# Linear attention in a fused decoder: row-by-row waits at its end, later unpackings, the context's low parts all on VectorE, and another order at its start

## The reference

```
qkv = silu(h @ qkv_w.T)                      # 32 heads of 128, q, k, v
scores = (q @ k.T) * decay                   # within and across blocks of 32 tokens
attn = scores @ v                            # 32 heads
xf = attn * rsqrt(mean(attn*attn) + 1e-5)    # over all 4096 columns of a token
x = x + (sigmoid(h @ gate_w.T) * norm_w * xf) @ out_w.T
...
x = x + cross_attention(layernorm(x), ctx, ctx, Wq, Wk, Wv, Wo)
x = x + layernorm(x) @ unpack_3bit(weight_q3, weight_norm).T + bias
```

## Time and profile before

| | us |
|---|---|
| median of 3 runs | 2436.48 |
| lowest and highest | 2434.27, 2437.48 |
| the profiled execution | 2437.57 |
| its span | 2435.0 |
| PE busy | 2323.7 (95%) |
| DVE busy | 1467.1 (60%) |
| ACT busy | 1020.6 (42%) |
| POOL busy | 914.8 (38%) |

### The profile page before, as it was taken

The page is one execution under the profiler, slowest core; times in us unless marked ns, Lnnn a source line. Parts: engine busy times, 40 slices in busy tenths (PEclk is TensorE's granted clock), DMA queues, the critical chain, the costliest instruction groups (busy, mean ns, idle before and its releaser), DMA issues.

```text
span 2435.0 us, 39959 instructions
## 1 busy us (share of the span) xinstructions
PE 2323.7 (95%) x12939; PEld 1972.7 (81%) x12939; DVE 1467.1 (60%) x3222; ACT 1020.6 (42%) x2447; POOL 914.8 (38%) x674
## 2 busy tenths in 40 slices
PE   6999899999999999998979999999999999987898
PEld 5788788888888888887768888888888888876556
DVE  7444644444444444446676666666666666658777
ACT  2111344444444444443244444444444444433784
POOL 3444523222222322221444444444444444413462
PEclk8999999999999999999989999999999999998999
DMA  3210212111111211110111111111111111120000
GB/s 118 78 43 26 96 53 83 55 52 65 55 52 52 81 56 52 65 56 27 55 52 46 45 45 45 45 45 45 45 45 45 46 46 45 45 95 18 1 1 35
DMA packets 39377, 125.26 MB, mean 51 GB/s; under 512 B 4888, under 2 KB 7320, under 8 KB 39328
## 3 DMA queue, kind: packets, MB, share of 16 engines
q1 hardware_dynamic: 39328, 124.64, 14.9%
HBM read 120.43 MB, written 4.19 MB: 51 GB/s over the span
## 4 chain that ended last, share of the span: by engine, by line
PE 81%; DVE 7%; POOL 5%; issue 4%; ACT 3%; DMA 0%; ACTq 0%; POOLq 0%; DVEq 0%; SPq 0%
PE pj L762 14%; PE pj L763 14%; PE pj L764 14%; PE ou L762 6%; PE ou L764 6%; PE ou L763 6%; PE tp L762 3%; PE tp L764 2%; PE tp L763 2%; PE sc L1101 2%; PE pv L952 2%; PE sc L936 2%; PE pv L1113 2%; POOL w_lo L550 1%; POOL sums_lo L644 1%
## 5 line engine op out<-in xcount | busy, mean ns | idle before, releaser
L550 POOL TENSOR_TENSOR w_lo<-raw,w_hi 128x1024 fp32r<-128x1024 f32 x100 | 240.6, 2407 | 802.2 <-ACT w_hi L1462 762.8
L762 PE MATMUL ou<-w_hi,act_hi 128*128 128x512 f32 x684 | 278.2, 407 | 11.8 <-DVE act_lo L2381 4.4
L1879 DVE TENSOR_TENSOR x<-x,ou 128x512 f32<-128x512 f32 x192 | 130.7, 683 | 247.6 <-PE ou L764 247.3
L763 PE MATMUL ou<-w_lo,act_hi 128*128 128x512 f32 x684 | 269.3, 394 | 0.0
L764 PE MATMUL ou<-w_hi,act_lo 128*128 128x512 f32 x684 | 269.2, 394 | 0.0
L762 PE MATMUL pj<-xt_hi,w_hi 128*128 128x512 f32 x622 | 254.2, 409 | 10.3 <-DVE values L2361 3.7
L763 PE MATMUL pj<-xt_lo,w_hi 128*128 128x512 f32 x622 | 244.7, 393 | 0.0
L764 PE MATMUL pj<-xt_hi,w_lo 128*128 128x512 f32 x622 | 244.4, 393 | 0.0
L1538 ACT ACTIVATE queries_keys<-pj 128x512 f32<-128x512 f32 x128 | 76.5, 598 | 244.8 <-PE pj L764 244.8
L762 PEld LDWEIGHTS ou<-w_hi,act_hi 128*128 128x128 f32 x684 | 130.0, 190 | 51.5 <-issue 18.5
L629 POOL TENSOR_TENSOR w_lo<-raw,w_hi 128x768 fp32r<-128x768 f32 x48 | 88.7, 1848 | 184.8 <-ACT w_hi L1599 184.6
(11 more groups left out here) (363 smaller groups left out, 6333.3 us busy)
## 6 DMA issues: line engine op xcount, KB each, us to landing
raw<-in_l1a_w SPq DMA_DIRECT2D x80, 512.0 KB, 3.4
raw<-in_l0x_w SPq DMA_DIRECT2D x64, 512.0 KB, 4.3
side<-in_side SPq DMA_DIRECT2D x32, 512.0 KB, 4.0
raw<-in_ffn_w SPq DMA_DIRECT2D x15, 512.0 KB, 3.4
raw<-in_l0f_w SPq DMA_DIRECT2D x6, 512.0 KB, 3.8
raw<-in_l1x_w SPq DMA_DIRECT2D x6, 512.0 KB, 3.4
raw<-in_taylor_w SPq DMA_DIRECT2D x5, 512.0 KB, 8.3
decay<-in_decay SPq DMA_DIRECT2D x16, 129.0 KB, 2.1
```

The lines of the kernel that those rows point to most:

```text
L550: pool.tensor_tensor(WL[:, s, :], RAW[:, s, :], f32(WH[:, s, :]), ALU.subtract).then_inc(w_ready[s], 1)
L762: pe.matmul(out, wh, xh, start=first, stop=False)
L763: pe.matmul(out, wh, xl, start=False, stop=False)
L1879: dve.tensor_tensor(dst, dst, ou[bank][:], ALU.add).then_inc(x_done, 1)
```

## The change

It has two places. **At the end**, PE's last odd half gets an order of its own: R4 stands behind V(0), R5 behind V(2), R6 behind V(3), R7 behind O(3), where all four stood behind V(3) and O(3) before. The tail's V(n) waits for its own value row instead of for R7, and `sums(0)` for R6. ACT and DVE follow with their parts; ACT rounds the context's pieces among and behind the value rows. DVE makes all four low parts of the context, behind R7's product, and POOL none. Of the unpackings, 0 and 1 stay in the odd half; 2 and 3, 4 and 5, 6 and 7 go behind the tail's `gated` of its batch rows 0, 1 and 2. SP starts the context's loads after the 63rd gate sigmoid instead of the 64th. DVE waits for the last gate weighting before it overwrites the third probabilities.

**At the start**, POOL makes the low sums of slot 3 first and begins `first_weights(1)` only when DVE has made two of the four low parts of the tokens (la_tlo); the clearing of the sums of squares goes behind slot 2's split. DVE normalises batch rows 6 and 7 one step earlier. ACT does `sums_hi(3, 0)` between the roundings of batch rows 6 and 7.

On SP and POOL:

```diff
-            sp.wait_ge(la_gs, 4 * HG)
+            sp.wait_ge(la_gs, 4 * HG - 1)
...
             pool.wait_ge(ou_full, OU["l0f"] + B)
+            sums_lo(3, 0)
+            pool.wait_ge(la_tlo, 2)
             first_weights(1)
-            pool.wait_ge(ln_x, 4 * B)
+            sums_lo(4, 0)
+            split(2, SLOT["l1a"][2])
             pool.memset(SQ[:], 0.0).then_inc(y_zero, 1)
-            sums_lo(3, 0)
-            split(2, SLOT["l1a"][2])
-            sums_lo(4, 0)
...
-            for c in range(2):
-                ctx_lo_again(c)
```

On PE, in `l1a_odd` and in the tail:

```diff
+                if not new:
+                    V(0)
+                    R(4)
+                    O(0)
+                    V(1)
+                    scores_l1a(i, 1, (la_fm, values + 1))
+                    O(1)
+                    V(2)
+                    R(5)
+                    O(2)
+                    V(3)
+                    R(6)
+                    O(3)
+                    R(7)
+                    return
...
-                    weighted(HG - 1, 1, n, event(HG - 1, "R7"))
+                    weighted(HG - 1, 1, n, event(HG - 1, f"R{4 + n}"))
...
             tail("V", 0)
+            pe.wait_ge(la_fm, event(HG - 1, "R6") + 1)
             sums(0)
```

On ACT, in `l1a_odd` and at the start:

```diff
                     V(0)
+                    row_value(i, 4)
                     V(1)
                     V(2)
-                    row_value(i, 4)
+                    row_value(i, 5)
+                    whole_ctx(0)
                     V(3)
-                    row_value(i, 5)
-                    act.wait_ge(c2_in, 16 * KC)
-                    for c in range(KC):
-                        act.activation(CH[:, c, :], CR[:, c, :], ACT.Copy).then_inc(c2_hi, 1)
-                        if c in (1, 3):
-                            row_value(i, 6 + c // 2)
+                    row_value(i, 6)
+                    whole_ctx(1)
+                    row_value(i, 7)
+                    whole_ctx(2)
+                    whole_ctx(3)
...
-            rows_hi(3, (6, 7))
-            row_value(None, 3)
+            rows_hi(3, (6,))
             act.wait_ge(x_saved, 32)
             act.wait_ge(ln_x, 4 * B)
             sums_hi(3, 0)
+            rows_hi(3, (7,))
+            row_value(None, 3)
```

On DVE, in `l1a_odd`, at the start and in the tail:

```diff
                     V(0)
+                    value_row(i, 4)
+                    widen()
                     O(0)
-                    widen()
...
+                    value_row(i, 7)
+                    for c in range(KC):
+                        lower_ctx(c)
...
+            row(3, 6)
             token_sums(4)
             row_lo(3, 4)
-            row(3, 6)
+            row(3, 7)
             token_sums(5)
             row_lo(3, 5)
-            row(3, 7)
...
-            for v in range(4, 8):
-                unpack(v)
...
             for n in range(HB):
                 gated(HG - 1, 1, n)
+                if n < 3:
+                    unpack(2 + 2 * n)
+                    unpack(3 + 2 * n)
```

More of the change, by code:

```diff
@@ L689, in _ @@
             split_lo(2, SLOT["l1a"][2] + HG - 1)
-            def ctx_lo_again(c):
-                pool.wait_ge(c2_hi, c + 1)
-                pool.tensor_tensor(CL[:, c, :], CR[:, c, :], f32(CH[:, c, :]), ALU.subtract).then_inc(c2_ready, 1)
             def both_heads(hf):
@@ L1684, in l1a_odd, with whole_ctx @@
                 if p is None:
+                    def whole_ctx(c):
+                        act.wait_ge(c2_in, 16 * KC)
+                        act.activation(CH[:, c, :], CR[:, c, :], ACT.Copy).then_inc(c2_hi, 1)
                     V(0)
+                    row_value(i, 4)
                     V(1)
                     V(2)
-                    row_value(i, 4)
-                    V(3)
-                    row_value(i, 5)
-                    act.wait_ge(c2_in, 16 * KC)
-                    for c in range(KC):
-                        act.activation(CH[:, c, :], CR[:, c, :], ACT.Copy).then_inc(c2_hi, 1)
-                        if c in (1, 3):
-                            row_value(i, 6 + c // 2)
+                    row_value(i, 5)
+                    whole_ctx(0)
+                    V(3)
+                    row_value(i, 6)
[3 more added lines that the diff above has]
+                    whole_ctx(3)
                     return
@@ L2430, in l1a_odd, with lower_ctx @@
                 if p is None:
-                    V(0)
+                    def lower_ctx(c):
+                        dve.wait_ge(c2_hi, c + 1)
+                        dve.tensor_tensor(CL[:, c, :], CR[:, c, :], f32(CH[:, c, :]), ALU.subtract).then_inc(c2_ready, 1)
+                    V(0)
+                    value_row(i, 4)
+                    widen()
                     O(0)
-                    widen()
                     V(1)
@@ L2439, in l1a_odd @@
                     decayed(i, 1, 1)
-                    value_row(i, 4)
+                    value_row(i, 5)
+                    unpack(1)
                     O(2)
                     V(3)
+                    dve.wait_ge(la_gw, i * 4 + 4)
                     decayed(i, 1, 2)
                     decayed(i, 1, 3)
-                    value_row(i, 5)
-                    unpack(1)
-                    O(3)
[L2448 to L2453, removed]
+                    value_row(i, 6)
+                    O(3)
+                    value_row(i, 7)
+                    for c in range(KC):
+                        lower_ctx(c)
                     return
```

## The result

The changed kernel takes 2422.2 us (median, 2417.79 to 2423.74) against 2434.27 (2430.73 to 2437.48) for the kernel before, run on the same chip beside it: a ratio of 0.9945, 95% interval 0.9932 to 0.9959. Run once more beside other kernels it gave 2419.86, ratio 0.9933 (0.9920 to 0.9946). The forecast was 2424.8, in a range of 2419.5 to 2431.5. The profiled execution after has a span of 2419.7 us and a time of 2422.34.

A forecast was written before the change was run, and what follows sets the result against it. PE was taken as the bound, with its waits at linear attention's two ends set by DVE and POOL taking turns. End -9.4 and start -2.3 sum to -11.7 us: median 2424.8 from 2436.48, range 2419.5 to 2431.5.

The forecast's parts named there:

- forecast 9.3: Last odd half, O(0) to R7's end: value rows moved into PE's waits and a higher clock take 9.3 us off.
- The clock's term of 2.9: Last odd half: with R4 filling half the 3.09 wait, the clock stays up, 2.9 us off; bound from below 0.
- the walk: R7's end to values_turned(0): ACT, POOL and both_heads(0) become the late chain; PE idles 11.6 us before sums(0).
- The charge of 1.3: Tail: unpackings 6 and 7 stand ahead of DVE's scaled additions and cost 1.3 us, bounds 0 and 2.5.
- the chain without slack: Tail: from DVE's scaled additions over the layer norm to PE's transposes, where PE had waited only 0.65 us.
- its wait in front of the transposes: Sign to look for at the layer norm: PE's wait before its transposes grows by about 1 us.
- first step: Start: POOL sleeps until two low parts are made; row 7's turning 2.5 us earlier, first product of sums 5.5.
- the price of slot 1's weights beside DVE's queries: Start: POOL's eight us make each SBUF-only query product wait for a turn; 4.5 us left at the third product.
- Rival A: The end's wait changes its place, POOL and ACT delay sums(0), the start gives nothing: -6 us, 2430.5; chance 0.18.
- B: Rival: no turn-taking at either end and PE warm through the start: -17.5 us, 2419.0; chance 0.10.
- C: Rival: slower, as ACT waits for the context pieces between R5 and V(3): +6 us, 2442.5; chance 0.03.
- D: Rival: no change; low clock in the odd half despite R4, A's delays, start +1: about -1.5 us, 2435.0; chance 0.07.

The follow-up runs named there:

- e_start: Only the start's edits, with the end as in the kernel before: 2429.19 us, ratio 0.9975 to the kernel before.
- e_r4_late: The changed kernel with R4 behind O(0) on PE instead of ahead of it: 2424.11 us, ratio 0.9951 to the kernel before.
- e_heads_lo0: Changed kernel with both_heads(0) ahead of POOL's split_lo, ACT's context roundings earlier, DVE's low part 0 ahead of row 7's product: 2417.93 us, ratio 0.9929.
- e_unpack0: The changed kernel with DVE's unpackings 2 to 7 all behind the tail's first gating: 2422.55 us, ratio 0.9943 to the kernel before.

## Why the prediction was right, and where its sizes were off

**The odd half of the end.** From O(0) to the end of R7, 23.5 us before, it is 2181.74 - 2167.68 = 14.1 after: 9.4 off, forecast 9.3. Each part shows: R4 fills the 3.09 but for 1.08 behind it and 0.35 ahead of it (it waits for DVE's last product of values, so its input was not quite there), the 2.83 in front of O(3) is 0.28, and the clock is 1.00. The clock's term of 2.9 measures 2.6: O(0) to V(2) is the same work in both kernels and takes 7.75 before, at 0.63, and 5.14 after, at 1.00. How long the clock stays low behind that wait is not fixed, though: e_start, with the old order here, pays 1.6 for it and so does e_r4_late. So about one us of the agreement is luck of the two profiles.

**R7's end to `values_turned(0)`.** 14.9 before, 13.25 after, so 1.7 off, forecast 1.4. The mechanism is the one of the walk, a wait of 10.93 where I had 11.6, ended by `both_heads(0)`, and POOL's two subtractions take 6.45 because they let DVE pass. Two steps of the walk were a little long (POOL begins 3.6 behind R7's end, not 4.4, and DVE's low part of the gating, 0.35, delays nothing) and three short (the two subtractions 6.4, not 5.9; `both_heads(0)` to `sums(0)` 1.6, not 1.3; `sums(0)` at half clock 1.7, not 1.5). Together 11.1 instead of 10.7.

**The charge of 1.3** for unpackings 6 and 7 was right in kind and too high. They make DVE's chain 1.2 late, 0.5 comes back at the variance's epsilon, and 0.75 is left at the transposes, counted from V(1). I had called the chain without slack; it has 0.2, where the output addition waits for PE. PE pays the 0.75 elsewhere than I said: its wait in front of the transposes, which I wanted to see grow by about 1, fell from 0.65 to 0.29, but it now waits 0.48 for `both_heads(1)` in front of `sums(1)`, where it hadn't waited, and 0.2 in front of the output product before that. In this pair of profiles the charge is hidden: from VT to V(1) PE took 0.8 less than before, since its clock came back sooner (5.76 against 6.59). That was not in the forecast, and it isn't a gain of the change either: the six profiles with the change's order there take 5.5 to 7.1.

**The start** was right in its first step (POOL idles 6.7 us until the second low part of the tokens, as the prediction had it) and wrong in what is given back. Row 7's turning came 2.4 earlier, forecast 2.5. The first product of sums: 5.5 forecast, 5.4 measured. At the product of the earlier trace rows that had waited 1.40, 2.5 forecast and 4.9 measured; at the last 2.3 forecast and 4.9 measured. The step that was mis-sized is the price of slot 1's weights beside DVE's queries: I let every SBUF-only product wait for a long turn. In the profile after:

```profile
1234.33 1.09 DVE L2377 TENSOR_TENSOR queries_keys<-side,queries_keys 128x512 f32<-128x512 f32 x1
...
1237.57 0.80 DVE L2377 TENSOR_TENSOR queries_keys<-side,queries_keys 128x512 f32<-128x512 f32 x1 [0.76 <-ACT side L1632]
...
1240.33 0.81 DVE L2377 TENSOR_TENSOR act_lo_whole<-side,act_lo_whole 128x512 f32<-128x512 f32 x1 [0.76 <-ACT side L1632]
...
1242.50 0.97 DVE L2377 TENSOR_TENSOR act_hi_whole<-side,act_hi_whole 128x512 f32<-128x512 f32 x1 [0.16 <-ACT side L1632]
```

Against some 0.68 alone that is 0.4, 0.1, 0.1 and 0.3: most of DVE's work there reads PSUM, only one instruction in three has both inputs in SBUF, and POOL's own are short (0.61 to 2.33). The product that had waited 1.40 for slot 4's low sums now waits 1.70, so ACT's rounding of slot 4's sums costs little more than before.

**Sum.** Of the two profiles: -11.1 to VT, -0.8 by the clock up to V(1), +0.8 for the unpackings, -4.9 at the start: -16.0 against the forecast's -11.7. On the profiled execution's 2437.57 that makes 2421.6, and it took 2422.34. The terms miss by 4.3 together, 2.6 of it at the start; that the first comparison of medians showed 12.1, so near to 11.7, is luck, the second showed 16.5. Rival A is half true and no rival: the wait did change its place, but its price was in the forecast. B is nearer in size (-17.5) with the wrong reason, since the turns are there. C is out: the context's pieces land 5.3 after their issue and ACT never waits for them. D is out with the clock.

## What to carry to other kernels

When a long wait is removed, look at the chain that ends next and at what stands ahead of it on its queue: a short instruction whose input is long there (`both_heads(0)`, 1.3 us) behind two long ones kept 5.3 us, nearly half of what the whole end had gained. Where DVE and POOL both work on SBUF alone, count how many POOL instructions fall inside DVE's chain, not only how early each can start; in e_heads_lo0 an earlier start of POOL cost a us. A short wait of PE that can be filled with a product ahead of its place is worth the product (1.4 here) and the low clock behind the wait (1.6 to 2.6), and whatever stands behind that product on the other engines (1.4). And when positions are compared across profiles, count from behind the last stretch at low clock: a price of 0.75 was lost in a spread of 1.5 until it was counted from V(1).

## What was unexpected of the hardware

- **Turns, in whole instructions.** Low parts of 1.2 us on DVE beside 2.4 us subtractions on POOL: four took 6.78 with one passing, three took 7.80 with two. Before this I had only the earlier trace rows. The parts that nothing passed took 1.22, the others 3.4. What passes depends on which issues first: the same two queues, shifted by a us, gave one more pass.
- **A tiny instruction can pay as well.** DVE's 128x4 `tensor_scalar` took 0.17 in the changed kernel and 0.65 in e_unpack0, where it ended with POOL's subtraction (2215.01 and 2214.97). The next of its kind meets a subtraction of POOL (2230.39 to 2232.77) in the changed kernel as well and takes 1.92, from 2230.88 to 2232.80.
- **The clock behind a short wait is not the same each time.** In front of row 7's turning PE waited 2.01 us both in the changed kernel and in e_start. The windows behind it, after first and e_start second:

```profile
1219.64:1222.00 2.36, 2.36 (x18) 2.27 (x19) 1.61 (x5) 2.15 (x5) 0.40 (x1) 1.00 0.00 0
```

```profile
1214.62:1217.00 2.38, 2.38 (x11) 2.38 (x12) 1.64 (x5) 2.09 (x4) 0.42 (x1) 0.50 0.00 0
```

The granted clock is 1.00 in one and 0.50 in the other, and 18 matmuls against 11 were begun in 2.4 us. Of the twelve profiles with the new start, which all wait 1.99 to 2.02 there, four have 0.50 behind it and eight 1.00. Here it cost nothing, since DVE set the next product: S1 is at +16.4 in both.
